# Moving the window stores and the mlp operand loads from ScalarE's queue to SyncE's in a seven-pass graph network

## What is computed

```python
# one of the seven passes, in essence
msg = table[src]                        # gather one row for each edge
msg = f(msg, edge data)                 # spline: times 4 coefficients; mlp: relu(P[src] + Q[dst] + E @ W)
agg = segment_sum(msg, dst, nodes)      # sum by destination
# mlp layer
msg_in = concat([nodes[row], nodes[col], edge_features])
aggregated = segment_sum(relu(msg_in @ mW1 + mb1) @ mW2 + mb2, col)
```

## Time and profile before

| | us |
|---|---|
| median of 3 runs | 18406.39 |
| lowest and highest | 18391.19, 18420.13 |
| the profiled execution | 18421.62 |
| its span | 18419.8 |

### The profile page before, as it was taken

One profiled execution on the slowest core, in us unless ns is written; L12 is line 12 of the kernel. 1 busy time (PEld: TensorE's weight loads), 2 busy tenths in 40 slices (PEclk: granted clock), 3 DMA queues, 4 the chain that ended last, 5 costly groups with the idle time before them and its releaser, 6 DMA issues.

```text
span 18419.8 us, 140081 instructions
## 1 busy us (share of the span) xinstructions
PE 8265.0 (45%) x34014; PEld 7031.2 (38%) x34014; DVE 4686.9 (25%) x7726; ACT 1222.7 (7%) x3388; POOL 11786.9 (64%) x11663
## 2 busy tenths in 40 slices
PE   7646565544444333334555543334424334333344
PEld 4434444333333333333444443333323333233333
DVE  4334433333443111112333331111121111211111
ACT  2101111000000000000111110000000000000000
POOL 0377666577776666665666656666656666566666
PEclk9877777777776555556777765555555555555555
DMA  4445554333333111113333321111111111111111
GB/s 193 168 125 164 159 157 153 113 100 105 102 104 85 25 32 32 32 33 81 100 101 99 99 78 25 26 26 26 26 26 26 26 25 26 27 26 27 27 28 26
DMA packets 901415, 1315.37 MB, mean 71 GB/s; under 512 B 434717, under 2 KB 592702, under 8 KB 875726
## 3 DMA queue, kind: packets, MB, share of 16 engines
q0 software_dynamic: 426240, 764.57, 17.1%
q1 hardware_dynamic: 272622, 372.40, 5.8%
q10 hardware_dynamic: 202464, 177.49, 3.3%
HBM read 965.86 MB, written 347.67 MB: 71 GB/s over the span
## 4 chain that ended last, share of the span: by engine, by line
another core or an unknown queue 52%; issue 16%; PE 15%; DVE 7%; POOL 6%; ACTq 1%; DMA 1%; DVEq 1%; ACT 1%; SPq 0%; POOLq 0%
PE PS L774 8%; POOL BIG L613 6%; PE PS L694 4%; DVE OH L1406 2%; DVE BIG L1419 1%; PE PS L807 1%; PE PS L768 1%; PE PS L703 1%; DVE BIG L1426 1%; DVE BIG L1434 1%; ACTq L982 0%; ACTq L983 0%; PE PS L681 0%; DMA AG<-acc 0%
## 5 line engine op out<-in xcount | busy, mean ns | idle before, releaser
L613 POOL DMA_INDIRECT BIG<-t_mp,IDX x4995 | 4914.0, 984 | 2565.7 <-issue 1766.2
L774 PE MATMUL PS<-BIG,OH 128*128 128x64 f32 (+3 forms) x23310 | 5614.5, 424 | 1468.5 <-DVE BIG L1419 684.6
L774 PEld LDWEIGHTS PS<-BIG,OH 128*128 128x128 f32 x23310 | 5002.7, 294 | 1954.4 <-issue 1395.1
L613 POOL DMA_INDIRECT BIG<-t_cell,IDX x3330 | 3603.0, 1082 | 2278.5 <-issue 1823.6
L768 PE MATMUL PS<-STG,CARRY 128*128 128x64 f32 (+3 forms) x1554 | 557.1, 457 | 6877.8 <-issue 2937.0
L1406 DVE TENSOR_TENSOR OH<-REL,IOTA 128x640 f32<-128x640 f32 x2331 | 1907.2, 822 | 4790.6 <-remote 3911.1
L768 PEld LDWEIGHTS PS<-STG,CARRY 128*128 128x128 f32 x1554 | 356.5, 285 | 7053.3 <-issue 3803.2
L613 POOL DMA_INDIRECT BIG<-t_p,IDX x1665 | 1655.7, 994 | 910.1 <-issue 517.5
L613 POOL DMA_INDIRECT BIG<-t_gcn,IDX x1665 | 1613.0, 969 | 832.4 <-issue 536.1
L1404 DVE TENSOR_SCALAR CARRY<-IOTA,DELTA 128x128 f32<-128x128 f32 x777 | 231.4, 298 | 3539.8 <-remote 2839.3
L1419 DVE TENSOR_TENSOR BIG<-BIG,COEF 128x1280 f32<-128x1280 f32 x666 | 989.7, 1486 | 454.9 <-DMA BIG<-t_cell,IDX 440.5
(11 more groups left out here) (151 smaller groups left out, 3416.9 us busy)
## 6 DMA issues: line engine op xcount, KB each, us to landing
t_cell<-BIG SPq DMA_DIRECT2D x198, 1280.0 KB, 4.4
BIG<-in_dst_row ACTq DMA_DIRECT2D x333, 240.0 KB
BIG<-t_mp,IDX POOLq DMA_INDIRECT x4995
BIG<-t_cell,IDX POOLq DMA_INDIRECT x3330
BIG<-t_gcn,IDX POOLq DMA_INDIRECT x1665
BIG<-in_ef ACTq DMA_DIRECT2D x333, 80.0 KB
BIG<-t_p,IDX POOLq DMA_INDIRECT x1665
BIG<-t_q ACTq DMA_DIRECT2D x333, 48.0 KB
```

The source lines that it names most:

```text
L613: nc.gpsimd.indirect_dma_start(to[:, j, :], None, table, bass.IndirectOffsetOnAxis(ap=IDX[:, at, column:column + 1], axis=0)).then_inc(gat ...
L774: last = nc.tensor.matmul(WIN[:, 0:out_w], OH[:, s % CHUNKS, j * P:(j + 1) * P], src[:, j, :], start=False, stop=(s % CHUNKS == CHUNKS - 1 ...
```

## The change

`store_window` and `load_mlp` are taken out of ACT's program and put into SP's, with their waits, their reading of the window's base (`value_load`) and their DMAs. ACT keeps `stage_window` and the copies of index lists. SP's loop now follows the units in every pass (`edged_units`). In spline and sum passes SP stores group g in the last slot of that group, so before slot 0 of the next unit. In the mlp pass SP issues the loads of a slot once the chunk before has its hidden product and its one-hot, and stores group g - 1 in the second slot of group g.

```diff
+                def load_mlp(c, to):
+                    sp.dma_start(RR[to][0:QW, :], t["dst_row"][0:1, bass.ds(c * CT * P, CT * P)]
+                                 .to_broadcast([QW, CT * P])).then_inc(rr_in[to], 16)
+                    sp.dma_start(SZ[to][QW:P, :], t["ef"][:, bass.ds(c * CT * P, CT * P)]).then_inc(ef_in[to], 16)
+                    at = sp.value_load(WBASE[0:1, bass.ds(c, 1)], min_val=0, max_val=z.nodes)
+                    sp.dma_start(QM[to][0:QW, :], t_q[bass.ds(at, QW), :]).then_inc(q_in[to], 16)
+
+                def store_window(g):
+
+                    sp.wait_ge(win_staged, gb + g + 2)
+                    hold(sp)
+                    at = sp.value_load(WBASE[0:1, bass.ds(g * CHUNKS, 1)], min_val=0, max_val=z.nodes)
+                    sp.dma_start(acc[bass.ds(at, P), :], STG[:, 0:acc.shape[1]]).then_inc(sums_landed, 16)
...
+                    if kind == "mlp" and not (last and s + AHEAD >= SLOTS):
+                        at = u * SLOTS + s
+                        if not (first and s == 0):
+                            sp.wait_ge(oht_ready, at)
+                            hold(sp)
+                            sp.wait_ge(hid_done, at)
+                            hold(sp)
+                        load_mlp(at + AHEAD, (c + AHEAD) % CHUNKS)
+                    if kind == "mlp" and c == 1 and not (first and gi == 0):
+                        store_window(g - 1)
+                    if kind != "mlp" and c == 2:
+                        store_window(g)
...
-                if kind == "spline":
-                    edged_units(sp, body, node)
-                else:
-                    with sp.Fori(0, z.steps - TAIL) as k:
-                        for s in range(SLOTS):
-                            node(s, k)
+                    for c in range(AHEAD):
+                        load_mlp(c, c)
+                edged_units(sp, body, node)
+                if kind == "mlp":
+                    store_window(z.groups - 1)
...
-                        store_window(g)
...
-                    if not (left == 0 and s + AHEAD >= SLOTS):
-                        at = u * SLOTS + s
-                        if not (first and s == 0):
-                            act.wait_ge(oht_ready, at)
-                            act.wait_ge(hid_done, at)
-                            hold(act)
-                        load_mlp(at + AHEAD, (s + AHEAD) % CHUNKS)
```

More of the change, by code:

```diff
@@ L976, in stage_window @@
                     nc.scalar.activation(STG[:, 0:out_w], WIN[:, 0:out_w], copy).then_inc(win_staged, 1)
-                def store_window(g):
-                    act.wait_ge(win_staged, gb + g + 2)
-                    hold(act)
-                    at = act.value_load(WBASE[0:1, bass.ds(g * CHUNKS, 1)], min_val=0, max_val=z.nodes)
-                    act.dma_start(acc[bass.ds(at, P), :], STG[:, 0:acc.shape[1]]).then_inc(sums_landed, 16)
                 def copy_list(g, to):
@@ L993, in next_list @@
                         copy_list(g + RING, h * UNIT + gi)
[L995 to L1000, removed]
                 def relu(u, s):
@@ L1044, in fast_pass @@
                 if kind == "mlp":
[L1045 to L1048, removed]
                     paired_units(act, mlp_body, node)
@@ L1051, in fast_pass @@
                     stage_window(z.groups - 1)
-                    store_window(z.groups - 1)
                 else:
```

## The result

The changed kernel takes 18505.63 us (median of 3 runs, 18504.42 to 18525.48) against 18406.39: a ratio of 1.0058, interval 1.0035 to 1.008. It is slower by 99 us, outside the 0.2% in which nothing could be told. The forecast was 18356, faster; the time lies inside the range, near its upper end. The profiled execution has a span of 18502.6 us, 82.8 more than the one before.

The account below looks back on a forecast made before the run. POOL's gathers bound every pass, so edits count only through POOL's waits. Terms -80 + 25 + 5 = -50 us from 18421.62 gave 18371.6; with that execution 15.2 above the median, forecast 18356, range 18200 to 18540.

Parts of the forecast that it names:

- Part 1: Mlp pass: without ACT's store the relu starts 1.2 us sooner, mostly reaching POOL: -80 us, bounds 0 and -236.
- the mlp gain is hidden: Rival, mlp pass: POOL bounds every pass, so -80 becomes -10 and the time is 18426 us; chance 0.28.
- Part 2: Mlp pass: ACT loses three loads a chunk, 1.9 us mostly fitting between relus; on SP they start no later: 0 us.
- Part 3 in passes 0 and 1: SP's store precedes the load of sums, issued 4.0 us later; about 10% reaches the end: +25 us.
- the 264 us at stake: Passes 0 and 1: upper bound if all the load of sums' delay reached the end, 33 steps x 2 passes x 4.0.
- Part 3 in the sum passes: Passes 4 to 6, pass 2 included: later load of sums holds PE up 1.3 us a burst: +5 us, bounds 0 and +129.
- SP slow at its steps: Rival: SP's sequencer steps take about 700 ns, delaying stores and loads; 200 us more, 18556 us; chance 0.22.
- Its deciding point: Slow SP would decide the outcome once its steps behind the window copy average over about 0.4 us.
- The checks named in the prediction: PE's relu waits and mlp pass fall about 80 us; pass 0's DVE wait grows 100 or more; other passes within 15.
- the sign of being wrong: Prediction wrong if the mlp pass gets no shorter, or passes 2 and 4 to 6 change over 30 us each.

Follow-up runs that it names:

- loads only: Against the kernel before, only the mlp operand loads move from ACT to SP, stores stay on ACT: 0.9992 (16401 us chip), 0.9998 (18266 us chip).
- wait only: Kernel before, no DMA changing engine; outside the mlp pass the load of sums waits until the unit's last store lands: 1.0011 (16401 us chip), 1.0024 (18266 us chip).
- load first: Changed kernel with each unit's last store moved behind slot 0's load of sums outside the mlp pass; against kernel before: 0.9993 (16401 us chip), 1.0011 (18421 us chip).
- the second pair: Kernel before and whole changed kernel, both unedited, profiled again on the 18421 us chip: 18411.64 us and 18488.3 us (1.0033).
- stores only: Against the kernel before, only the window stores move to SP, mlp loads stay on ACT: 0.9986 (16401 us chip), 1.0048 (18266 us chip).

## Why the prediction was wrong

**The bound** was read rightly in the main: an edit reaches the end through POOL's waits, and on the chip without such waits no edit moved more than 0.14%. (One reading was off: PE is busy for 56% of pass 0 in the earlier trace rows, so idle for less than half of it.)

**Part 1 (-80)** is the step that failed. Its first half held only in part. Where the store alone was taken from ahead of the relu, PE's waits for the relu fell by 112 us; in the whole change they fell by 77 in the mlp pass (70 over the whole span) in the first pair of profiles, but by 10 over the whole span in the second, and the two profiles of the kernel before differ by 39. Its second half, "I let most through", had no row behind it. POOL's waits being short and many was read as following this chain ("under 3 us each" is their mean; the longest is 6.9 in the earlier trace rows). The run with the store behind the relu shows that they do not: -112 us of PE's waits, -2 of POOL's, a total of 0.9997, whose interval leaves at most 22 of the 80 us. The rival "the mlp gain is hidden" was right on this step; what POOL's waits there do follow was not found. The same text let 10% through in pass 0, by POOL's share of waits, and nearly all here; 10% of 80 would have been -8.

**Part 2 (0)** held in the total: the loads only give 0.9992 and 0.9998, both intervals over 1. A few us may stand behind it: with the loads on SP the mlp pass is 6 to 10 us longer wherever POOL waits, and POOL waits 12 to 19 us more in it (409.8, 421.2 and 419.7 against 392.6 and 407.5; loads only 387.6 against 368 to 373). Joining the queues moved no limit: together they held 5.8 + 3.3 = 9.1% of the 16 engines before and hold 9.0% now, for the same 549.89 MB. The Trainium skill says in DMA: Bandwidth & Descriptors, section Issuing engines are not separate DMA queues, that DMAs started by different engines run on the same 16 DMA engines and that starting them from several saves only sequencer time; these shares agree.

**Part 3 in passes 0 and 1 (+25)** named the right mechanism and was sized too small, in three terms. The delay: the load of sums was to be issued 2.5 us after the window copy; it is 4.8 in pass 0, where SP has the edge attributes' load besides the coefficients', and 4.1 in pass 1. The share that comes through: pass 0 grew by 50 and 38 us in the two pairs of profiles, and DVE's wait in it by 81 and 149, so about 60% and 25% and not a tenth; pass 1's wait grew by 150 and 252 us and the pass by 4 and 14. Over both passes that is 54 of 231 us and 52 of 401, 23% and 13%: the 264 us at stake were of the right size, and the error of the two passes together is under 30 us. The gaps between passes, +24 and +46 us, were in no sum; they went back to 1260 when the load of sums came first, and all four profiles with the load behind the last window (1285 to 1306) lie above the five without (1248 to 1279), so they hang on the order too. The order as a whole is worth 38 to 44 us (wait only) or 46 us (whole change against load first) of 67 to 99.

**Part 3 in the sum passes (+5)** held in size, though not by its reasoning. The load of sums comes 5.5 to 6.3 us after the copy instead of 2.7, DVE's waits in passes 4 to 6 rose from 33.7 to 689.3 us, and each of those passes is 2 us longer, pass 2 8 shorter; the second pair has -3 to +3, so nothing beyond the scatter. The step from 129 us before the 11% to +5 has no working: 11% of 129 is 14.

**SP slow at its steps** was half right. Its deciding point was steps of over 0.4 us on average behind the window copy. 2.80 us less 0.3 for the copy, over the seven steps that the trace has ahead of the DMA, is 0.36 us (ACT's were 0.12), near that point, and the store starts 1.7 us later than ACT's did. It was priced at 200 us, and this is not what it cost. In pass 0 the slow stores are mostly those of a unit's first two groups (3.57 us after the copy on average), which have no load of sums behind them; the last one, with the load of sums behind it, starts after 1.61 us, before 1.26. And with the load of sums first, stores as late cost 0.11% (interval -0.02 to +0.23), of which the mlp pass shows +10 us.

**Added up.** From the forecast's -50 us to the measured +99 (+67 the second time), 80 are part 1, which brought nothing. Part 3's +30 became 38 to 46 for the order. The 21 to 61 us that are left over are stores and loads issued by SP beyond their order; the runs don't split them further.

**The checks named in the prediction:** PE's waits for the relu -77 (as said, but -10 the second time, over the whole span); the mlp pass +7 and not shorter (the sign of being wrong); DVE's wait in pass 0 +81 and +149 (100 or more was said); passes 1, 2, 4, 5 and 6 within 8 us; pass 0 +50, outside the 15.

**What stays open.** By the ratios the stores only cost 88 us where the wait only costs 44, and their intervals touch only at 1.0034: about half of what the stores cost on that chip is not the order. It may be that SP's slow steps lengthen the chain that the order made, but the profiled execution of the stores only was the shortest of its runs and doesn't show where the difference is. Whether the +7 and +10 us of the mlp pass come from SP's late loads was not settled. Nor was what ends the quiet stretches of the earlier trace rows, in which the slow steps lie. No kernel tried beats the kernel before by more than 0.14%.

## What to carry to other kernels

A wait that an edit shortens is worth what the bounding engine's waits lose, not what the waiting engine gains: take one factor for it, from rows, and use it for gains and losses alike. Before a step goes to another queue, list every step already there that has to come behind it: here the load of sums behind one store cost 38 to 46 of 67 to 99 us, and issuing it first brought that back. A small edit on the old engine (the wait alone, the store behind the relu) tells an order's price from an engine's in one run. Profile the same kernel twice before a difference between two profiles is read: here 70 us of waiting less became 10 in the second pair.

## What was unexpected of the hardware

The same kernel takes 16401, 18266 and 18406 to 18421 us on the chips met here. In the profiles almost all of that is POOL waiting inside the passes (1943 us in the kernel before on the first chip; in the four kernels profiled on the chip at 16401 no gap within a pass is over 0.32 us). The granted clock doesn't explain it: in passes 2 and 4 to 6 it is 0.50 (1.2 GHz) on both, and they take 2398 to 2400 us against 2114 to 2122 with the stores only. Slow sequencer steps go with it: SP steps of 650 to 760 ns are 974 of 5799 in the kernel before, 2221 of 16161 in the changed one, 1 of 11840 on the chip at 16401. ACT, which had 183 of 13805 such steps before, has 0 of 4189 after the change. The slow steps went with the work to SP: there are more of them, though a smaller share of SP's steps (14% against 17%). What makes them slow was not found.
